# One core, PE-bound mixture-of-experts block: silu joined on DVE, routing weights on POOL, and gate and up begun ahead of the routing

## The reference

```python
x = x + attn_a(layernorm(x))     # 8 heads of 16 channels; softmax over channels
x = x + ffn(layernorm(x))
x = x + attn_b(layernorm(x))     # one head over 512 tokens, banded sigmoid on the scores
x = x + ffn(layernorm(x))

def ffn(h):                      # 8 experts of 336 hidden units
    probs = softmax(h @ router_w.T)
    k = argmax(clip(gelu(h @ actor_w1.T + b1) @ actor_w2.T + b2, -30, 30)) + 1
    scores = where(rank(probs) < k, probs, 0)
    for e in range(8):
        y = (silu(h @ gate_w[e].T) * (h @ up_w[e].T)) @ down_w[e].T
        out = out + scores[..., e:e+1] * y
    return out
```

## Time and profile before

| | us |
|---|---|
| median of 3 executions (539.32 to 540.28) | 539.7 |
| the profiled execution | 539.46 |
| its span, first to last instruction | 537.7 |
| PE busy in it | 507.8 (94%) |
| DVE, ACT, POOL busy | 349.4, 245.9, 280.9 |
| mean granted clock of PE | 0.977 |

### The profile page before, as it was taken

One profiled execution on the slowest core, in us unless ns is written; L12 is line 12 of the kernel. 1 busy time (PEld: TensorE's weight loads), 2 busy tenths in 40 slices (PEclk: granted clock), 3 DMA queues, 4 the chain that ended last, 5 costly groups with the idle time before them and its releaser, 6 DMA issues.

```text
span 537.7 us, 6464 instructions
## 1 busy us (share of the span) xinstructions
PE 507.8 (94%) x2056; PEld 350.3 (65%) x2056; DVE 349.4 (65%) x770; ACT 245.9 (46%) x406; POOL 280.9 (52%) x268
## 2 busy tenths in 40 slices
PE   3777999999999999999989999899998999999996
PEld 2465767677767667677656677566765677666663
DVE  3457765474399988689984798938958263733332
ACT  3434562534653657337654356642755335332221
POOL 4123655565555466555664436544455454665553
PEclk9688999999999999999989999989999999999999
DMA  8500000000000000000000000000000000000000
GB/s 270 171 2 0 2 0 1 1 0 1 0 2 0 2 0 2 0 0 2 1 1 0 1 0 2 1 0 1 20 2 0 0 12 10 1 0 22 0 0 20
DMA packets 7773, 7.37 MB, mean 14 GB/s; under 512 B 700, under 2 KB 7612, under 8 KB 7740
## 3 DMA queue, kind: packets, MB, share of 16 engines
q1 hardware_dynamic: 7740, 6.97, 4.1%
HBM read 5.91 MB, written 1.05 MB: 13 GB/s over the span
## 4 chain that ended last, share of the span: by engine, by line
PE 85%; DVE 9%; issue 2%; ACT 1%; DMA 1%; POOL 1%; SPq 0%; DVEq 0%; POOLq 0%
PE bank L991 24%; PE bank L865 15%; PE bank L867 15%; PE bank L866 15%; PE bank L1037 3%; PE bank L892 1%; PE bank L959 1%; PE bank L1028 1%; PE bank L882 1%; PE bank L910 1%; DVE t L809 1%; DMA w<-in_w 1%; PE bank L935 1%; DVE xn L681 1%; DVE gt L775 1%
## 5 line engine op out<-in xcount | busy, mean ns | idle before, releaser
L485 POOL TENSOR_TENSOR t<-t,sl 128x512 f32<-128x512 f32 x168 | 218.2, 1303 | 203.3 <-DVE t L809 182.9
L809 DVE TENSOR_TENSOR t<-bank,sbc 128x512 f32<-128x512 f32 x168 | 114.7, 685 | 118.1 <-PE bank L867 116.2
L991 PE MATMUL bank<-t,WD 128*128 128x512 f32 x336 | 173.0, 598 | 0.0
L582 ACT ACTIVATE sl<-bank 128x512 f32<-128x512 f32 x168 | 99.7, 597 | 151.9 <-PE bank L867 126.7
L865 PE MATMUL bank<-xhF,WGh 128*128 128x512 f32 x168 | 106.8, 636 | 0.1
L991 PEld LDWEIGHTS bank<-t,WD 128*128 128x128 f32 x336 | 64.0, 190 | 16.8 <-issue 1.0
L865 PE MATMUL bank<-xhF,WUh 128*128 128x512 f32 x168 | 67.7, 403 | 3.4 <-DVE t L809 3.2
L867 PE MATMUL bank<-xhF,WUl 128*128 128x512 f32 x168 | 67.4, 401 | 0.0
L866 PE MATMUL bank<-xlF,WUh 128*128 128x512 f32 x168 | 67.2, 400 | 0.0
L867 PE MATMUL bank<-xhF,WGl 128*128 128x512 f32 x168 | 66.6, 397 | 0.0
L866 PE MATMUL bank<-xlF,WGh 128*128 128x512 f32 x168 | 66.5, 396 | 0.0
(11 more groups left out here) (160 smaller groups left out, 672.6 us busy)
## 6 DMA issues: line engine op xcount, KB each, us to landing
stage<-in_gate SPq DMA_DIRECT2D x7, 192.0 KB, 5.7
stage<-in_up SPq DMA_DIRECT2D x7, 192.0 KB, 6.0
WD<-in_down SPq DMA_DIRECT2D x7, 192.0 KB, 6.0
X<-in_x SPq DMA_DIRECT2D x4, 256.0 KB, 5.3
out<-X SPq DMA_DIRECT2D x4, 256.0 KB, 2.3
raw<-in_small SPq DMA_DIRECT2D x1, 580.0 KB
rows<-in_row SPq DMA_DIRECT2D x1, 136.0 KB, 5.4
cols<-in_columns SPq DMA_DIRECT2D x1, 3.0 KB
```

Source lines behind the costliest of these rows:

```text
L485: pool.tensor_tensor(t2[k % NT2][:, :], t2[k % NT2][:, :], sl[k % NSL][:, :], ALU.mult).then_inc(a_done, 1)
L582: act.activation(sl[k % NSL][:, :], bank[k % 2][:, :], ACT.Silu).then_inc(silu_done, 1)
L809: dve.tensor_tensor(t2[k % NT2][:, :], bank[2 + k % 2][:, :], sbc[k // CH % 2][:, :], ALU.mult).then_inc(t2_done, 1)
L991: pe.matmul(OACC[:, :], WD[:, c, :], t2[k % NT2][:, :], start=(c == 0), stop=(c == CH - 1))\
```

## The change

DVE now multiplies up by silu, and POOL multiplies the result by the routing weights. So DVE's product of a chunk (a step `uk` of its own) waits for the silu and no longer for `sbc`; POOL's (`um`) waits for `sbc` and no longer for the silu; the silu of chunk k waits for DVE's product of k-2 where it waited for POOL's. `t2` has twelve tiles. `gu` and `uk` of chunk 0 begin once the routing's `xl` is in the list, and the products of POOL and the downs are put in by a function that follows POOL's estimated load: a down at least 1.6 steps after its product, up to two of each per k. The routing of batch 0 gets tighter offsets of its own and starts 4 steps ahead of chunk 0. The attention A of batches 0 to 3 starts at -26, -16, 0 and 17, where it was -42, -26, 1 and 21.

```diff
-LAG = 3
-NSL, NT2 = 2, 6
+AFTER_POOL = 1.6
+NSL, NT2 = 2, 12
-A_STARTS = (-42, -26, 1, 21)
+A_STARTS = (-26, -16, 0, 17)
-GU_AFTER = {("tanh", 0): 0, ("act", 0): 1}
+F0_STEPS = [(0, "stats"), (1, "xn"), (2, "xT"), (3, "xl"), (4, "route"), (4, "rexp"), (4, "inner", 0),
+            (5, "inner", 1), (5, "rsum"), (6, "rrank"), (6, "tanh"), (6, "gelu"), (7, "act"),
+            (8, "actk"), (9, "sbc")]
+F0_START = -4
+POOL_COST = dict(um=1.35, stats=1.4, ass=.8, bqkl=1.4, actk=1.1, inner=1)
...
+        if s[0] in POOL_COST:
+            pool_free[0] = max(pool_free[0], k) + POOL_COST[s[0]] / 2.25
...
+    def products(k, most):
+        for _ in range(most):
+            j = len(um_end)
+            if ("uk", j) in done and ("sbc", j // CH) in done and pool_free[0] < k + 1:
+                add(("um", j))
+                um_end.append(pool_free[0])
+            if downs[0] < len(um_end) and um_end[downs[0]] + AFTER_POOL <= k:
+                add(("down", downs[0]))
+                downs[0] += 1
...
-        if k + 1 < 0 or (k + 1) % CH or ("sbc", (k + 1) // CH) in done:
+        if k + 1 < 0 or (k + 1) % CH or ("xl", "F", (k + 1) // CH) in done:
             k += 1
...
-        if k >= 0 and ("um", k) not in done:
-            if k >= 2:
-                add(("gu", k))
-            add(("um", k))
-            if k >= LAG:
-                add(("down", k - LAG))
+        if begins:
+            add(("gu", k))
+            assert k < NT2 or ("down", k - NT2) in done
+            add(("uk", k))
+        if k >= 0:
+            products(k, 2)
...
-                    pool.wait_ge(silu_done, k + 1)
-                    pool.tensor_tensor(t2[k % NT2][:, :], t2[k % NT2][:, :], sl[k % NSL][:, :], ALU.mult).then_inc(a_done, 1)
+                    pool.tensor_tensor(t2[k % NT2][:, :], t2[k % NT2][:, :], sbc[k // CH % 2][:, :], ALU.mult).then_inc(a_done, 1)
...
-                        act.wait_ge(a_done, k - NSL + 1)
+                        act.wait_ge(t2_done, k - NSL + 1)
...
-                if kind == "um":
+                if kind == "uk":
                     k = s[1]
-                    if k % CH == 0:
-                        wait_free(dve, turn_of["sbc", k // CH])
                     dve.wait_ge(u_full, k + 1)
+                    dve.wait_ge(silu_done, k + 1)
-                    dve.tensor_tensor(t2[k % NT2][:, :], bank[2 + k % 2][:, :], sbc[k // CH % 2][:, :],
+                    dve.tensor_tensor(t2[k % NT2][:, :], bank[2 + k % 2][:, :], sl[k % NSL][:, :],
                                       ALU.mult).then_inc(t2_done, 1)
```

More of the change, by code:

```diff
@@ L148, in plan @@
     last = CH * 2 * NB
-    threads = [thread("F", n, F_STEPS, CH * n - F_AHEAD) for n in range(2 * NB)]
+    threads = [thread("F", n, F_STEPS, CH * n - F_AHEAD) if n else thread("F", 0, F0_STEPS, F0_START)
+               for n in range(2 * NB)]
     threads += [[CH * (n + 1) + 3, [(0, ("yT", n))], 0] for n in range(2 * NB - 1)]
@@ L156, in plan @@
     debt = [0.0, 0.0]
+    pool_free = [0.0]
+    um_end, downs = [], [0]
     def ready(s):
@@ L185, in add @@
             free_after.extend([by] * TURNS[s[0]])
+    def products(k, most):
[7 more added lines that the diff above has]
+                downs[0] += 1
     k = A_STARTS[0] - 1
     while k < last - 1:
-        if k + 1 < 0 or (k + 1) % CH or ("sbc", (k + 1) // CH) in done:
+        if k + 1 < 0 or (k + 1) % CH or ("xl", "F", (k + 1) // CH) in done:
             k += 1
+            begins = k >= 0
         else:
+            begins = False
             for th in threads:
                 th[0] -= th[0] <= k
-        if k >= 0 and ("um", k) not in done:
-            if k >= 2:
-                add(("gu", k))
-            add(("um", k))
-            if k >= LAG:
-                add(("down", k - LAG))
+        if begins:
[4 more added lines that the diff above has]
+            products(k, 2)
         pe = 2.2
@@ L214, in plan @@
                 add(s)
-                if s in GU_AFTER:
-                    add(("gu", GU_AFTER[s]))
                 pe, act, dve = pe + cost[0], act + cost[1], dve + cost[2]
@@ L221, in plan @@
     assert not any(th[1] for th in threads)
-    for k in range(last, last + LAG):
-        add(("down", k - LAG))
+    while downs[0] < last:
+        k += 1
+        products(k, 2)
     add(("yT", 2 * NB - 1))
@@ L482, in _ @@
                     k = s[1]
+                    if k % CH == 0:
+                        wait_free(pool, turn_of["sbc", k // CH])
                     pool.wait_ge(t2_done, k + 1)
-                    pool.wait_ge(silu_done, k + 1)
-                    pool.tensor_tensor(t2[k % NT2][:, :], t2[k % NT2][:, :], sl[k % NSL][:, :], ALU.mult).then_inc(a_done, 1)
+                    pool.tensor_tensor(t2[k % NT2][:, :], t2[k % NT2][:, :], sbc[k // CH % 2][:, :], ALU.mult).then_inc(a_done, 1)
         @block.scalar
@@ L574, in _ @@
                     if n >= 2:
-                        act.wait_ge(t2_done, CH * (n - 1))
+                        act.wait_ge(a_done, CH * (n - 1))
                     act.activation(sbc[n % 2][:, :], m_bank(t)[:, :], ACT.Copy).then_inc(n_free(t), 1)
```

## The result

The changed kernel takes 563.0 us (median of 4, 561.46 to 566.6), the kernel before on the same chip 539.99: ratio 1.0435, interval 1.0394 to 1.0477. So it is slower, as forecast, but by 23 us, not by 9, and outside the range. The profiled execution took 566.6 (span 564.8), 3.6 above the median, so sums from its rows come out large by about that much.

What follows compares the result with a forecast made beforehand. PE's idle time in the first 60 us, set by a chain of waits, was taken as the bound. `sbc` at 67 less 46.8, less 6.5 done early, less 4.7 saved, gives +9.0: 548.7 us median, range 541 to 554.

Steps and rivals of the forecast that it cites:

- The head: Order ahead of chunk 0 and routing among the first chunks: `sbc` at 67 instead of 46.80, net +9.0 us.
- the lower bound, 65.0: Earliest time in us for `sbc` by the worked steps, at full clock, 18.2 later than 46.80; total +7.0 (546.7).
- the 1.5 for chunk 0 and `route` at low clock: Ahead of `act`: 1.5 us added if PE runs chunk 0 with `route` at low clock.
- 2.5 of it foreseen for low clock: Stretch from `act` to chunk 5: 2.5 us added if PE runs it at low clock.
- 2 in all: Low-clock allowance taking `sbc` from 65.0 to 67; chunk 0 1.5, `act` stretch 2.5 and later `y` 2.3 make 71.3.
- The middle: After `sbc`, PE hardly idle up to 160 us; from 160 on, no more than 3 us different from before.
- From there it has downs and chunks in store and stops no more: PE after `sbc`: stops no more, so the 4.7 us lost after 46.80 are saved.
- the sign set for it: Forecast wrong if the middle, from 160 us on, differs from before by more than 3 us.
- where the layer begins a new pass, 21 chunks wait in the same order as before: Later pass starts: same waiting order as before, given no cost of its own.
- Swap alone: Rival, dense middle: DVE's product waits for silus behind 18 loads; six reaching PE add 7.8 us, 556.5; chance 0.07.
- Filling the waits: Rival, head: early chunks fit the routing's waits, `sbc` at 53.9, net -4.1 us, 535.6; chance 0.13.
- the break-even of the sum: Head: `sbc` at 58.0 us decides; earlier than that the change gains.

Runs made afterwards that it cites:

- e5: The kernel before with batch 1's attention 10 steps behind batch 0's instead of 16 (start -32 for -26): 548.40 us.
- e2: The changed kernel with attention starts and batch 0's routing offsets of before, all ahead of chunk 0; swap, twelve buffers and new placing of downs stay: 550.59 us.
- e18: The kernel before with POOL's first product behind every `rstd` held until DVE has done the `xn` of that norm: 546.02 us.
- e13: The changed kernel with POOL's first product behind each `rstd` held until DVE has done that `xn`: 560.57 us.
- e15: The changed kernel with batches 2 and 3 started as before, chunk 0 behind `rexp`, old order ahead of it, products held until `xn` except attention B's norms: 544.22 us.
- e17: The changed kernel with batches 2, 3 started as before, chunk 0 behind `rexp`, old order ahead, passes 1 to 7 gated on `sbc`, products held behind every norm: 543.38 us.
- e6: The changed kernel with the attention of batches 2 and 3 started as before (1 and 21 for 0 and 17): 555.6 us.
- e11: The changed kernel with passes 1 to 7 gated on `sbc` as before, pass 0 still on `xl`: 562.13 us.
- e1: The kernel before with only the two factors swapped between DVE and POOL; order, six buffers and lag 3 as before: 541.08 us.
- e12: The changed kernel with attention and routing in the order of before, passes after the first gated on `sbc`, chunks 2 and 3 moved into PE's waits: 547.79 us.

## Why the prediction was wrong

**The head, right in mechanism, short in size.** Worked out, with what came in brackets, were `simT` at 22.1 (22.18), routing's transposes at 37.6 to 39.9 (38.46), chunk 0's gate at about 40 (41.08), `gt` and `gelu` ending with 57.4 (60.63), PE idle some 4 us ahead of `act` (4.80), `sbc` from 65.0 to 71.3, 67 taken (71.95). (The hand sum for the routing's transposes, given as 6.6 us after `y`, adds up to 6.5; it changes nothing.) From the lower bound, 65.0, to 71.95 are 6.95: the routing's transposes come 0.9 after 37.6, `act` another 3.0 after its 57.45 (half of that the 1.5 for chunk 0 and `route` at low clock), and from `act` to `sbc` it takes 10.6 instead of 7.55, another 3.0 (2.5 of it foreseen for low clock). I had taken 2 in all, because idle stretches of 4 us are longer than any that stood ahead of low-clock work before, "but I would not count all three". Two of the three came in full: the clock from 40 to 50 us is 0.59, from 60 to 70 it is 0.56; only `y` was spared. That the idle stretches brought the low clock, as I argued, is not shown: from 40 to 50 us e5, with two stops of 4 us, has 0.50, but so has e2, without them, and e18, with the list of before, has 0.53. One execution of before, with 0.89 there, was too little to price the clock by.

**The middle, the failed step.** "From there it has downs and chunks in store and stops no more" was wrong, and the sign set for it, a middle that differs from before by more than 3 us, came: 9 to 12.6 us are lost after 36 us of work. The step took equal instructions and a full store for equal time. It held that "where the layer begins a new pass, 21 chunks wait in the same order as before", while the new gate begins a pass at `xl`; and it gave no price to the moved starts of attention of batches 2 and 3 once `sbc` is there, nor to the products that the list holds back for POOL. What the runs show in its place, by the lags of the changed kernel:

- 2.0 us between 36 and 80 us of work. POOL runs a row of products behind a norm's power, DVE's `xn` stands still for one product per step, and PE pays (1.71 us at 86.75). Shown by e13, e15 and e17, where the step is 0.0 to 0.2.
- 8.5 us from there to the down of chunk 89. The moved starts of batches 2 and 3 put more of DVE's other steps between two products, and PE waits for the product (2.80 us at 224.91). That the starts carry it is shown by e6 (2.4) and the groups above; the way is shown at this one place.
- 2.1 us from there to the end, where passes begun ahead of their weights make PE wait 2.38 us; 0.1 in e11.

**What stays open.** Each lag is one execution's, and part of it is the clock: behind the waits at 224.91, 300.37 and 406.94 the changed kernel has stretches at 0.50 to 0.51, while before has two such in its middle (from 277.8 and 349.5). DVE's other steps are longer beside POOL too: before the wait at 224.91 a `pr` that takes 0.19 alone took 1.06. Steps other than `xn` were not freed in any run, so what they add is argued, not shown.

**The rivals, and the loads.** Swap alone: 0.65% at most (e1). Filling the waits comes out even, not ahead: with `sbc` at 57.71 the head's lag is 0.3, near the break-even of the sum. On table loads the row was right: the Exp behind the load at 48.28 starts 1.29 us after it, the silu behind that at 50.62 too. The Trainium skill (ScalarE: Activation LUTs, What ACT_TABLE_LOAD costs) has 2.66 us for a switch; here the measurement decides.

## What to carry to other kernels

Work put ahead of a chain is free only in the engines' idle time, and each of the queues that carry the chain is in order: go through all of them, and read PE's clock in more than one execution before pricing it. A thread that an edit moves has to be priced at every place where its steps land, in the dense middle too: look for the longest run of other steps between two products in the queue of the engine that PE waits for. A bigger store between two engines changes when the second one runs, not only whether it waits: a backlog runs back to back, at the moment at which its release is also another engine's release. Where DVE and POOL both work on SBUF, look for DVE groups whose mean doubles (`xn` 1.1 us or 4.9) before putting down a middle as unchanged, and hold the work that has slack only where the awaited step comes next in its own queue.

## What was not expected of the hardware

DVE's scalar subtract-and-multiply on 128x128 in f32 (`xn`, four steps, 1.12 us alone) takes 2.08 us beside one product of POOL (before, at 373.38), 3.90 beside three (e12), 4.92 beside a row of six (changed): about one step per product. DVE's product that reads PSUM is not stretched: its mean is 685 ns in both kernels, and in the changed one it takes 0.68 at 86.62, inside POOL's row of six. PE's granted clock in the head differs between executions of one list: from 40 to 50 us it was 0.89 in before and 0.53 in e18, whose list is the same and whose hold touches no product ahead of 50 us.
